# The projection of the next sequence and exponential 7 change places in TensorE's repeated list

## The reference

```python
def reference(x, subject, zX, zY, zR, side, seq_len, label, ...):
    # L0: a linear map chosen by the sequence's subject
    x = x + (einsum('bnh,boh->bno', x, weight[subject]) + bias[subject][:, None, :])
    # L1: a reflecting Laplacian along both axes, and a reaction term
    x = x + (zX * lap_x(x) + zY * lap_y(x) + zR * x * (1.0 - x))
    # L2: attention of 16 heads; queries, and one "self" key and value, from side,
    #     keys and values from x, masked by seq_len
    q, k, v = (side + b_self) @ Wq + bq, (x + b_prev) @ Wk + bk, x @ Wv + bv
    weights = softmax(concat([mask(q @ k.T), q . k_self]) * SCALE)
    x = x + (weights @ concat([v, v_self])) @ Wo + bo
    # L3: three feed-forward experts (one chosen by label, two shared), mixed by a gate
    x = x + eo * w[0] + s0 * w[1] + s1 * w[2]
    return x
```

## Time and profile before

| what | value |
|---|---|
| median of 3 runs | 1010.71 us (1007.92 to 1014.98) |
| the profiled execution | 1012.89 us |
| its span, first to last instruction | 1011.1 us |
| mean granted TensorE clock | 0.984 of full speed |
| TensorE, matmul records | 976.6 us, 97% |
| VectorE, ScalarE, GpSimd | 795.6, 685.5, 638.2 us |

### The profile page before, as it was taken

How to read it: one execution, slowest core, us unless ns; L and a number is a source line. 1 busy time by engine, 2 the same in 40 slices (tenths; PEclk the granted TensorE clock), 3 DMA queues, 4 the chain that set the end, 5 groups by cost and what they waited for, 6 DMA issues and landing times.

```text
span 1011.1 us, 27951 instructions
## 1 busy us (share of the span) xinstructions
PE 976.6 (97%) x9604; PEld 929.4 (92%) x9604; DVE 795.6 (79%) x1558; ACT 685.5 (68%) x1443; POOL 638.2 (63%) x546
## 2 busy tenths in 40 slices
PE   7879999999999999999999999999999999999896
PEld 7669999999999999999999999999999999999796
DVE  6877878878788787878878787887878788888533
ACT  5666858667685876768587676857767685776541
POOL 5767747576684757658575765856576585656450
PEclk9889999999999999999999999999999999999988
DMA  6533142223213222331322223132232313221110
GB/s 175 171 104 107 50 112 72 63 84 100 88 42 109 79 63 84 93 95 42 105 83 63 84 86 103 42 102 83 66 84 80 108 42 94 84 72 55 43 53 11
DMA packets 92029, 82.70 MB, mean 82 GB/s; under 512 B 12101, under 2 KB 90981, under 8 KB 92005
## 3 DMA queue, kind: packets, MB, share of 16 engines
q1 hardware_dynamic: 91572, 81.99, 27.8%
q10 hardware_dynamic: 432, 0.39, 0.2%
HBM read 52.59 MB, written 4.20 MB: 56 GB/s over the span
## 4 chain that ended last, share of the span: by engine, by line
PE 60%; POOL 17%; issue 15%; DVE 4%; ACT 2%; SPq 1%; DMA 1%; POOLq 0%; DVEq 0%
PE hid L653 6%; PE out L653 6%; PE out L654 6%; PE out L655 6%; PE hid L654 6%; PE hid L655 6%; POOL prob_lo L1427 5%; POOL exp_lo L1363 5%; PE front L775 4%; PE front L761 3%; PE front L653 3%; PE front L655 3%; PE front L654 3%; PE pv L716 2%; PE pv L717 2%
## 5 line engine op out<-in xcount | busy, mean ns | idle before, releaser
L653 PE MATMUL hid<-x_hi,exp_hi 128*128 128x256 f32 x768 | 231.3, 301 | 1.5 <-DVE x_lo L1251 1.5
L1427 POOL TENSOR_TENSOR prob_lo<-prob,prob_hi 128x512 f16<-128x512 f32 x143 | 184.5, 1290 | 72.2 <-ACT prob_hi L1011 72.2
L653 PE MATMUL out<-hid_hi,exp_hi 128*128 128x256 f32 x768 | 226.6, 295 | 0.1
L654 PE MATMUL hid<-x_lo,exp_hi 128*128 128x256 f32 x768 | 217.1, 283 | 0.0
L655 PE MATMUL hid<-x_hi,exp_lo 128*128 128x256 f32 x768 | 216.8, 282 | 0.0
L654 PE MATMUL out<-hid_lo,exp_hi 128*128 128x256 f32 x768 | 214.6, 279 | 0.0
L655 PE MATMUL out<-hid_hi,exp_lo 128*128 128x256 f32 x768 | 214.4, 279 | 0.0
L1363 POOL TENSOR_TENSOR exp_lo<-raw,exp_hi 128x512 fp32r<-128x512 f32 x128 | 168.9, 1335 | 70.2 <-ACT exp_hi L1028 70.2
L1171 DVE TENSOR_REDUCE s_max<-front 128x2 f32<-128x512 f32 x247 | 163.3, 688 | 61.8 <-PE front L761 59.9
L1050 ACT ACTIVATE hid_hi<-hid 128x512 fp32r<-128x512 f32 x192 | 114.8, 598 | 95.7 <-PE hid L655 94.7
L1007 ACT ACTIVATE prob<-front 128x512 f32<-128x512 f32 x246 | 147.5, 600 | 25.4 <-PE front L775 22.1
(11 more groups left out here) (241 smaller groups left out, 2332.9 us busy)
## 6 DMA issues: line engine op xcount, KB each, us to landing
raw<-in_wi SPq DMA_DIRECT2D x64, 256.0 KB, 3.8
raw<-in_wo SPq DMA_DIRECT2D x64, 256.0 KB, 2.8
q_rows<-w_raw SPq DMA_DIRECT2D x80, 128.0 KB, 2.4
k_rows<-x_raw SPq DMA_DIRECT2D x48, 128.0 KB, 2.4
k_rows<-x1T SPq DMA_DIRECT2D x45, 128.0 KB, 2.4
x_raw<-in_x SPq DMA_DIRECT2D x16, 256.0 KB, 2.9
w_raw<-in_w SPq DMA_DIRECT2D x16, 256.0 KB, 2.7
s_raw<-in_side SPq DMA_DIRECT2D x16, 256.0 KB, 3.6
```

Source lines behind the costliest of these rows:

```text
L653: nc.tensor.matmul(acc, w_hi, a_hi, start=first, stop=False)
L654: nc.tensor.matmul(acc, w_hi, a_lo, start=False, stop=False)
L1427: nc.gpsimd.tensor_tensor(prob_lo[:, h % NPROB, :], prob[:, h % NPROB, :], prob_hi[:, h % NPROB, :], ALU.subtract).then_inc(prob_split_poo ...
```

## The change

In TensorE's repeated list x1 is moved from behind E7 to in front of it, directly behind m1. No other list is changed, and no step is added or taken away. The lists of the opening keep their order.

```diff
 PE_BODY = """
 ...
-E0 S12 P4 E1 S13 H6 E2 S14 P5 E3 S15 H7 E4 E5 P6 E6 H8 m1 E7
-x1 P7 q E8 H9 E9 lap P8 E10 E11 H10 E12 kp E13 P9 E14 E15 H11 P10 pvend P11
+E0 S12 P4 E1 S13 H6 E2 S14 P5 E3 S15 H7 E4 E5 P6 E6 H8 m1 x1 E7
+P7 q E8 H9 E9 lap P8 E10 E11 H10 E12 kp E13 P9 E14 E15 H11 P10 pvend P11
```

## The result

The changed kernel takes 1013.62 us in the median of 22 runs, the kernel before 1011.08 in 22 runs beside it: a ratio of 1.0022, 95% interval 1.0013 to 1.0031, so about 2.2 us slower (the medians themselves lie 2.5 us apart). The profiled execution has a span of 1012.5 us.

A forecast was written before the change was run, and what follows sets the result against it. TensorE's own list was taken to bound the kernel. 13 turns at +0.16 us (+2.1) and -0.16 in the first gave +1.9, so 1010.71 + 1.9 = 1012.6 us; range 1006 to 1018.

The forecast's parts named there:

- The likeliest case: Whole kernel: x1's wait returns at q, +1.9 us, 1012.6 us for the median; chance 0.66.
- central step: At q on TensorE: q now waits for VectorE to sum x1 out of its bank, ending at q's old start, 526.09.
- The hole at x1 goes: TensorE ahead of x1: the wait for ScalarE's copy of m1 disappears, -0.24 us in each of 14 turns.
- The second switch to float32: TensorE behind E7, in front of P7: one more switch from bfloat16 to float32, +0.08 us per turn.
- the one turn in which nothing holds q: First loop turn: VectorE ends early, so q has no wait and TensorE comes 0.16 us earlier.
- The wait comes back at q: TensorE at q: q waits for VectorE's x1 in 13 turns, each +0.16 us, +2.1 in all.
- The price of the wait: At q: start 0.06 us behind VectorE's end, second matmul at 526.37 instead of 526.21, +0.16 us per turn.
- The restart: At q behind the wait: second matmul 0.22 us behind the first instead of 0.12, its weight load standing bare.
- the rival of a free restart: At q: weight load pulled ahead of the wait, +0.06 us per turn, +0.6 in all, 1011.3 us; chance 0.15.
- GpSimd's floor: At q: GpSimd's rest of s ends at 525.86, so q can't start before 525.91 whatever VectorE does; not binding.
- The late E7: E7 reaches ScalarE and VectorE later but is covered; behind the loop it is 0.61 us late, also covered: 0.
- The collision: VectorE ahead of x1: an instruction lengthened beside GpSimd's, 0.93 us more per turn, +15 us, 1025.6; chance 0.04.

The follow-up runs named there:

- the last experiment: Against the changed kernel, q waits first for the parts of s, then for x1's bank; ratio 1.0018 to the kernel before.
- the first experiment: Against the changed kernel, x1 in VectorE's list moved from behind H8 to in front of it; ratio 0.9977 to the kernel before.
- the control: Against the kernel before, x1 in VectorE's list moved in front of H8, TensorE's order unchanged; ratio 0.9991.
- E5: A step of the kernel, not a run; the changed kernel with VectorE's x1 before z and E5's rest measured ratio 1.0021 to the kernel before.
- another run: Against the changed kernel, VectorE's x1 before z and E5's rest, ScalarE's high part of s before m1's copy; ratio 0.9966 to the kernel before.

## Why the prediction was right

Forecast were 1012.6 us and +1.9; measured are 1013.62 and +2.2, ratio 1.0022. The likeliest case took place, and with it its central step.

- **The hole at x1 goes.** Right; it was 0.24 us by the prediction's count and counts for more. The next float32 matmul behind E7's second half starts 0.02 us behind it, not 0.12 (525.01 behind 524.99), so 0.34 us of the 0.36 were lost. The prediction's 0.24 was too small. The second switch to float32 costs its 0.08 (525.01 to 525.21). In the one turn in which nothing holds q this is seen: -0.34 + 0.08 = -0.26 by these rows, -0.24 measured, and not -0.16. In the 13 others the new hole takes it up, so there the error cost the forecast nothing.
- **The wait comes back at q.** Right, and shown from both sides: VectorE's read earlier by 0.61 us moves q to the second floor; later by 0.86 us moves q by 0.86; in the old order neither moves it.
- **The price of the wait.** The start was put 0.06 us behind VectorE's end and is 0.13. That is the term of the sum that was mis-sized: 13 x 0.07 = 0.9 us. The row was of a matmul that carries its wait, q's stood on an instruction ahead of it; the last experiment shows that this is the difference, and q behind GpSimd in the first experiment, whose wait the matmul carries, bears it out (0.05 to 0.06 in 13 turns). x1 in the kernel before had the same 0.13 behind m1's copy, and the prediction used it there; it took the wrong one of its two rows for q. The restart, 0.22 to the second matmul, was right (526.90 to 527.12), and so the rival of a free restart didn't take place. The Trainium skill, "TensorE: Matmul & The Clock Gate", section "Step-by-step: what each phase is for", says that TensorE pulls weight loads ahead of matmuls in flight. In the stream the trace agrees (the load at 526.28 for the matmul at 526.39); behind the wait it doesn't: q's load, which stands behind the waiting instruction in the program, starts at 526.89.
- **A part isn't charged.** q's second matmul is 0.25 us later, the turn 0.20 longer; 0.05 are given back at the Laplacian. In the kernel before it had a hole of 0.03 us and a restart, which a later TensorE no longer meets: its first matmul now stands 0.02 behind the exponential (530.63 behind 530.61), as in the control, where the same 0.05 go with q unmoved. The prediction had no such term.
- **Luck in the sum.** The mechanism was right, but 2.2 came so near to 1.9 because two misses offset each other: the price, +0.9 us, and the Laplacian, 13 x 0.05 = 0.65 us the other way.
- **GpSimd's floor.** Right in its place: 0.23 us ahead of VectorE's end in the changed kernel (526.54 against 526.77), and the next to hold q when VectorE didn't. That it stands "whatever VectorE does" was wrong: with E5's rest behind x1, GpSimd ended 3.24 us behind m1 instead of 3.63.
- **The late E7.** Right: covered on ScalarE (0.34 us left), on VectorE and behind the loop.
- **The collision.** It didn't happen in the changed kernel, and it was a real risk: four experiments met it, three at z, at up to 0.86 us a turn, and one at the reaction's sum (and at z by less, 0.53 us in place of 0.17).

## What to carry to other kernels

A wait that is removed by exchanging two steps of a ring of banks moves to the step that now follows in that bank. Before making the exchange, look when the reader of that bank is done by its own list: here it ended at the very moment at which the bank's next writer came, and the earlier producer bought nothing until the reader's place in its list was moved as well. Then count again what else is near, since two floors lay within 0.3 us of one another, and each move of one engine's small instruction changed which of GpSimd's it stood behind.

## What the runs showed of the hardware

- **A wait on an instruction of its own costs about 0.08 us more than one carried by the matmul or its load**: 0.13 from the releaser's end to the matmul in the one case, 0.05 in the other, with nothing but the order of the two waits changed, and alike in all of the 13 turns.
- **A weight load that stands behind a wait, or carries it, starts with its matmul** (526.89 and 526.90, 0.11 ahead in a stream), and the second matmul stands 0.22 us behind the first, 0.12 in a stream.
- **A VectorE instruction of eight elements took 1.04 us behind a GpSimd instruction** and ended with it, while x1's sum, from PSUM and one tile of SBUF, ran beside the same GpSimd instruction in its usual 0.87 in another run (523.18, GpSimd until 523.74). The Trainium skill, "SBUF — State Buffer", section "SBUF: two separate sides", states it: VectorE with two inputs from SBUF and GpSimd exclude each other for a whole instruction, and who starts first keeps the port. By that rule, the trace agrees: z's product and the reaction's sum read two tiles of SBUF, x1's sum one. It works the other way too: GpSimd's rest of s took 1.66 us behind VectorE's rest of E5 and 1.29 without it. The exclusion isn't quite whole in the rows: z, the reaction's sum and GpSimd's rest each ended 0.13 to 0.19 us earlier than the other's end plus their own length alone. Who starts first can turn within one run. In the run with ScalarE's s before m1, the gate product, which also reads two tiles of SBUF, took 0.48 us when it started 0.18 ahead of GpSimd, and 1.31 when it started 0.14 behind (528.62 against 528.48):

```profile
468.35 0.48 DVE L1270 SCALAR_TENSOR_TENSOR gate_terms<-gate,e_out,gate_terms 128x256 f32<-128x256 f32 x1
```

```profile
468.53 1.32 POOL L1427 TENSOR_TENSOR prob_lo<-prob,prob_hi 128x512 f16<-128x512 f32 x1 [1.11 <-ACT prob_hi L1011]
```
